# A Mamba block and a gated FFN on one core: the last batch's du*B of one group of four by GpSimd, the first batch's chain in halves, and a new order of all engines

## The chip, the cores and the metric

The kernel runs on one core of a Trainium2 chip, as one program of about 3400 instructions written by hand for each engine. The metric is the device time of one launch in microseconds (us): 197.79 us, the median of three runs (197.42 to 198.32). The engines are TensorE (PE, matrix products), VectorE (DVE), ScalarE (ACT), GpSimd (POOL) and SyncE (SP, which here issues all the DMAs).

## The reference

Four batches (BATCH = 4) of L = 256 tokens. The first layer is a Mamba block on a context of 128 features, with 256 inner channels, 16 states per channel and a convolution of 4 taps. Cut to what matters:

```python
x = einsum('bld,ed->bel', hidden_states, in_proj_w)
x = silu(causal_conv(x, conv_w) + conv_b)                 # u, 256 channels
dt_low, Bm, Cm = split(einsum('bdl,ed->bel', x, x_proj_w), [8, 24])
dt = softplus(einsum('brl,dr->bdl', dt_low, dt_proj_w) + dt_proj_b)
def step(state, inp):                                     # scan over the 256 tokens
    d, b, c, u = inp
    state = state * exp(d[..., None] * A) + (d * u)[..., None] * b[:, None, :]
    return state, einsum('bdn,bn->bd', state, c)
y = (scan(step) + D * x) * silu(z)                        # z = layernorm(x_in)
x_in = x_in + tanh(g_xattn) * swapaxes(y)
```

The second layer, on the sum, quantizes its layer norm per token to 8 bits, multiplies with `w13` (1408 x 256), forms `relu(x1)**2 * x3`, takes an RMS norm with weight, quantizes again, multiplies with `w2` (256 x 704), scales by tanh(g_ffn) and adds to the sum.

## The kernel before

The 256 inner channels are two halves (h = 0, 1) of 128 partitions; tokens lie along the free axis. The 16 states of a batch are worked in four groups, `k = 4 b + i` over the whole run. In batches 0 to 2 a group is 4 states on all 256 tokens. In batch 3 a group is 8 states on 128 tokens: groups 0 and 1 are tokens 0 to 127, groups 2 and 3 tokens 128 to 255, and the state at the cut is carried over (`edge`, `carry`).

Each group passes four engines, once for each half h, and these names stand for that everywhere below:

- `mixH` (PE, L959): du*B for all states of the group, written to PSUM (`m_ps`, two banks for each half and no second buffer), as a matmul of the transposed du with `bd`, diagonal blocks that hold B. In batches 1 to 3 `bd` is made by DMA: `bput` writes B's rows on the diagonal of a DRAM tensor, `bget` reads a group of it back (512 KB).
- `decayH` (ACT, L585): exp(dt*A) into `dA` (SBUF, two buffers).
- `scanH` (DVE, L783): the recurrence, from `dA` (SBUF) and `m_ps` (PSUM) into `hb` (SBUF, three buffers).
- `outH` (POOL, L356): hb times C, in place. C comes as `cs`, spread over all partitions by DMA (`cput` to DRAM, `cget` back, 512 KB a group).
- `sumH` (PE, L983): adds the states up in `y_ps` and transposes to tokens.

Ahead of a batch's groups runs the chain `ctxT`, `inproj` (PE), `tap` (ACT), `conv` (DVE), `sigm0` (ACT), `clamp` (DVE), `sigm1` (ACT), `u`, `xdbl` (PE), `lowc` (DVE), `dtproj` (PE), `absx`, `ln1q` (ACT), `series` (DVE), `cubic`, `dt` (DVE), `dtadd`, `du`, `duT` (PE and ACT), each on both halves in one instruction or one pair. After its groups come `yz`, `x1` (DVE) and the FFN: `center`, `absx1`, `quant1`, `xqT`, `up` (PE, L1013, 4 a batch), `relu`, `gate`, `gated`, `square`, `absmax`, `scale2`, `quant2`, `iqT`, `down` (PE, L1030), `final` and `store`. In batch 3 this is done for each 128 tokens alone. `w` are transposes of the FFN weights, with `w_hi`, `w_mid`, `w_res`, `w_lo` splitting each into three bf16 parts, and `warm` are PE transposes whose result is not used (L879).

Nothing is scheduled by a program: `PLAN` is a table written out by hand with one list for each engine, `name/batch.index` for each step, and each engine works its list strictly in order, waiting on semaphores. A step late in one list holds up all that stand behind it there. PE's outputs other than `m_ps` and `y_ps` share three PSUM banks in rotation (`claim`, `emptied`): a step waits until the one three fills ahead has been read.

```python
dve.wait_ge(dA_ok, HALVES * k + h + 1)
dve.wait_ge(m_full, HALVES * k + h + 1)
if k >= 3:
    dve.wait_ge(red_ok, HALVES * (k - 3) + h + 1)
```

## Time and profile before

| | |
|---|---|
| median of three runs | 197.79 us |
| the profiled execution: its time, its span | 197.55 us, 195.8 us |
| mean granted TensorE clock | 0.991 |
| PE, DVE, ACT, POOL busy | 177.1, 166.9, 152.2, 119.7 us |
| first scan starts, last matmul ends | 32.15 us, 193.03 us |

The profiled time is 1.75 us more than the span, which runs from the first to the last instruction. Busy time counts an engine's instructions alone; what it spends waiting for a semaphore is idle, and the rows show in brackets how long it was and who ended it. Matmuls are pipelined, so that a busy PE is one that has work in it. Rows of the timeline are merged stretches of like instructions and overlap by some tenths; rows of the chain are cut so that they do not. A fp32 matmul stands as two in the trace (x4 in a row is two of the program).

### The profile page before, as it was taken

What the parts mean: (1) busy time and instruction counts of PE and PEld (TensorE: products, weight loads), DVE (VectorE), ACT (ScalarE), POOL (GpSimd) and SP (SyncE); (2) the same over time, 40 slices, a digit from 0 to 9 for tenths busy, and PEclk for the clock granted to TensorE, in tenths of its full rate; (3) what the DMA queues carried; (4) which work ended last, traced back from release to release, by engine and by line L of the source; (5) the groups of instructions that cost most, each with busy time, mean ns of one, the idle gap of its engine ahead of it and who ended that gap; (6) DMA issues with size and microseconds to landing.
All of it is one profiled execution on the core that took longest, in us unless ns stands there. A gap on an engine that the chain in (4) does not pass through costs nothing.

```text
span 195.8 us, 3397 instructions
## 1 busy us (share of the span) xinstructions
PE 177.1 (90%) x1114; PEld 140.3 (72%) x1114; DVE 166.9 (85%) x260; ACT 152.2 (78%) x380; POOL 119.7 (61%) x83
## 2 busy tenths in 40 slices
...
GB/s 63 171 383 301 379 125 2 5 108 257 371 235 107 107 3 5 13 194 227 110 100 225 7 102 260 177 0 229 124 0 30 0 0 0 30 0 2 55 30 54
DMA packets 26498, 22.47 MB, mean 115 GB/s; under 512 B 15112, under 2 KB 19952, under 8 KB 26480
## 3 DMA queue, kind: packets, MB, share of 16 engines
...
## 4 chain that ended last, share of the span: by engine, by line
PE 52%; DVE 20%; issue 9%; POOL 9%; ACT 4%; SPq 2%; DMA 2%; DVEq 0%; POOLq 0%
PE m_ps L959 17%; PE w_ps L1013 12%; PE y_ps L983 10%; DVE hb L783 5%; POOL hb L356 5%; PE w_ps L1030 4%; DMA ctx_in<-in_ctx 2%; POOL dt L364 2%; PE w_ps L1021 2%; DVE gt L839 1%; POOL du L367 1%; PE w_ps L926 1%; PE w_ps L940 1%; POOL w13T L480 1%; PE y_ps L971 1%
## 5 line engine op out<-in xcount | busy, mean ns | idle before, releaser
L356 POOL TENSOR_TENSOR hb<-hb,cs 128x1024 f32<-128x1024 f32 x31 | 74.2, 2403 | 15.9 <-DVE hb L783 10.2
L783 DVE TENSOR_TENSOR_SCAN hb<-dA,m_ps 128x1024 f32<-128x1024 f32 x32 | 72.6, 2275 | 2.7 <-PE m_ps L959 2.0
L959 PE MATMUL m_ps<-bd,duT 128*128 128x256 f32 (+1 forms) x224 | 60.2, 413 | 2.3 <-issue 1.3
L585 ACT ACTIVATE dA<-dt,nega 128x255 f32<-128x255 f32 (+1 forms) x160 | 59.4, 452 | 0.0
L959 PEld LDWEIGHTS m_ps<-bd,duT 128*128 128x128 f32 x224 | 40.7, 190 | 14.1 <-issue 7.8
L983 PE MATMUL y_ps<-identf,hb 128*128 128x128 f32 x256 | 31.9, 273 | 2.4 <-POOL hb L356 2.4
L983 PEld LDWEIGHTS y_ps<-identf,hb 128*128 128x128 f32 x256 | 29.0, 141 | 5.1 <-POOL hb L356 2.8
L1013 PE MATMUL w_ps<-w13T,xqT 128*128 128x352 bf16 x192 | 30.4, 313 | 0.0
L1013 PEld LDWEIGHTS w_ps<-w13T,xqT 128*128 128x128 bf16 x192 | 18.6, 98 | 10.0 <-issue 0.9
L360 POOL TENSOR_TENSOR rr<-rr,q 128x512 f32<-128x512 f32 x2 | 2.9, 1470 | 24.1 <-DVE rr L739 24.1
L1030 PE MATMUL w_ps<-w2T,iqT 128*128 128x256 bf16 x144 | 16.7, 273 | 0.5 <-DVE ctx_in L856 0.5
L371 POOL TENSOR_TENSOR gw<-gg,normw 128x704 f32<-128x704 f32 x7 | 12.5, 1788 | 7.6 <-DVE gg L825 7.6
L705 DVE SCALAR_TENSOR_TENSOR xc<-w_ps,convw,xc 128x255 f32<-128x255 f32 (+2 forms) x24 | 9.6, 468 | 8.0 <-ACT xc L522 8.0
L1030 PEld LDWEIGHTS w_ps<-w2T,iqT 128*128 128x128 bf16 x144 | 13.8, 98 | 2.7 <-DVE ctx_in L856 0.8
L825 DVE SCALAR_TENSOR_TENSOR gg<-w_ps,finv,ru 128x352 f32<-128x352 f32 x16 | 9.0, 574 | 6.5 <-ACT ru L630 6.5
L627 ACT ACTIVATE ru<-w_ps,finv 128x352 f32<-128x352 f32 x16 | 8.7, 547 | 5.2 <-PE w_ps L1013 5.1
L646 ACT ACTIVATE iqT<-w_ps 128x384 bf16<-128x384 f32 x16 | 6.9, 481 | 4.1 <-PE w_ps L1021 4.1
L879 PE MATMUL y_ps<-identf 128*128 128x128 f32 x66 | 10.1, 314 | 0.0
L364 POOL TENSOR_TENSOR dt<-xs,lw 128x512 f32<-128x512 f32 x4 | 5.1, 1273 | 7.9 <-DVE lw L747 7.9
L879 PEld LDWEIGHTS y_ps<-identf 128*128 128x128 f32 x66 | 9.1, 165 | 0.7 <-issue 0.6
L620 ACT ACTIVATE xqT<-w_ps 128x512 bf16<-128x512 f32 (+1 forms) x5 | 2.5, 506 | 7.7 <-PE w_ps L1001 7.7
L630 ACT ACTIVATE ru<-ru 128x352 f32<-128x352 f32 x16 | 8.0, 497 | 0.5
...
## 6 DMA issues: line engine op xcount, KB each, us to landing
...
```

The source lines that it names most:

```text
L356: E.tensor_tensor(h_g, h_g, cs[:, s0:s0 + sn, l0:l0 + ln], ALU.mult).then_inc(hc_end if (b, i, h) == OUT_END else hc_ok[h], 1)
L364: E.tensor_tensor(dt[:, p], xs[:, :], lw[:, :], ALU.add).then_inc(dt_ok, 1)
L371: E.tensor_tensor(gw[:, p, i], gg[:, p, i], normw[:, :], ALU.mult).then_inc(gw_ok[i], 1)
L585: last = act_fn(dA_g[:, s, 1:ln], dt[:, p, h, l0 + 1:l0 + ln], ACT.Exp, scale=nega[:, h, s0 + s:s0 + s + 1])
L705: last = V.scalar_tensor_tensor(out=xc[:, h, s:L], in0=h_ps[:, h, 0:L - s], scalar=convw[:, h, TAPS - 1 - s:TAPS - s], in1=xc[:, h, s:L], ...
L783: V.tensor_tensor_scan(hb[:, k % 3, h], dA[:, k % 2, h].rearrange("p n l -> p (n l)"), m_ps[:, h], 0.0, ALU.mult, ALU.add).then_inc(scan_o ...
L825: V.scalar_tensor_tensor(out=gg[:, p, h, c * UC:(c + 1) * UC], in0=bank("up", b, i, 1)[:, 0:UC], scalar=finv[:, b, h:h + 1], in1=ru[:, p, ...
L879: T.transpose(y_ps[:, 0, 0:P], identf[:, :], identf[:, :])
L959: last = T.matmul(m_q[:, :, c * P - l0:(c + 1) * P - l0], duT[:, p, c, h * P:(h + 1) * P], bd[:, (s0 + sn // 2 * q) // GN, c, n0:n0 + sn / ...
L983: last = T.matmul(y_ps[:, t, h * P:(h + 1) * P], hb[:, k % 3, h, at:at + P], identf[:, :], start=False, stop=(s0 + s == NS - 1), is_transp ...
L1013: last = T.matmul(ps[:, 0:UC], xqT[:, kh, h, :], w13T[:, s, kh, c0:c0 + UC], start=(kh == 0 and s == 0), stop=(kh == 1 and s == 2))
L1030: last = T.matmul(ps[:, 0:DI], iqT[:, p, i, f, :], w2T[:, s, f * DI:(f + 1) * DI], start=(f == 0 and s == 0), stop=(f == FB - 1 and s == 2))
```

## The change

Three things change, and with the third nearly every line of the table.

1. Group 1 of batch 3 (8 states, tokens 0 to 127) loses its two mixes. SP writes 8 rows of B to DRAM (`mput`) and reads them back spread over all partitions (`mget`, two DMAs) into the part of `bd` that this group's diagonal blocks would have taken; the two `bget` of that part load half as much. POOL multiplies them with du into `hb` (`pm0`, `pm1`, 128x1024 each). ACT writes this group's decays into `m_ps` in place of `dA`, once the scan before has left it, and DVE scans from `m_ps` and `hb`, in place.
2. In batch 0 the chain from `inproj` to `duT` is cut into its two channel halves: `inproj/0.0`, `inproj/0.1` and so on for conv, clamp, u, dtproj, absx, ln1q, series, cubic, dt, dtadd, du, duT. Semaphores count with `tick`.
3. All five lists of `PLAN` stand in a new order.

The diff, cut to its core:

```diff
+PM = (None, None, None, 1)
...
+def by_pool(b, i):
+    return PM[b] == i
...
+def mixes(b, i, h):
+    return HALVES * sum((a, g) <= (b, i) and not by_pool(a, g) for a in range(BATCH) for g in range(NG)) + h - 1
...
+def halves(b, i):
+    return range(i, i + 1) if b == 0 else range(HALVES)
+def tick(b, i=HALVES - 1):
+    return i + 1 if b == 0 else HALVES + b
...
-        mix1/2.3 up/1.1 duT/3.0 up/1.2 down/0.0 mix0/3.0 mix1/3.0 up/1.3 szT/3.0 sum0/2.2 mix0/3.1 sum1/2.2 sum0/2.3
+        sum0/2.1 iqT/0.0 up/1.1 mix1/2.3 sum1/2.1 up/1.2 duT/3.0 sum0/2.2 mix0/3.0 up/1.3 mix1/3.0 sum1/2.2 sum0/2.3
...
+    b_dram = nc.dram_tensor("b_rows", (BATCH, NS, L), fp32, kind="Internal").ap()
...
+        def rows_of(b, i):
+            if b == BATCH - 1:
+                return bd[:, slots(b, i)[0]:slots(b, i)[-1] + 1, i // 2]
...
             elif name == "cubic":
-                eng.wait_ge(rr_ok, b + 1)
-                E.tensor_tensor(rr[:, :], rr[:, :], q[:, :], ALU.mult).then_inc(cubic_ok, 1)
+                eng.wait_ge(rr_ok, tick(b, i))
+                E.tensor_tensor(rr[:, hs], rr[:, hs], q[:, hs], ALU.mult).then_inc(cubic_ok, 1)
...
                 elif name == "bget":
                     sp.wait_ge(b_put, 16 * HALVES * b)
-                    sp.wait_ge(m_full, HALVES * (NG * (b - 1) + i + 1))
-                    sp.dma_start(bd[:, i], d_rows[:, :, GN * i:GN * (i + 1), :]).then_inc(b_got[i], 16)
+                    taken(b, i)
+                    cs_ = slice(0, HALVES)
+                    if b == BATCH - 1 and PM[b] is not None and i in slots(b, PM[b]):
+                        cs_ = slice(1 - PM[b] // 2, 2 - PM[b] // 2)
+                    sp.dma_start(bd[:, i, cs_], d_rows[:, cs_, GN * i:GN * (i + 1), :]).then_inc(b_got[i], 16)
+                elif name == "mput":
+                    s0, sn = group(b, PM[b])[2:]
+                    sp.wait_ge(free["dve"], emptied("xdbl", b, 0))
+                    sp.dma_start(b_dram[b, s0:s0 + sn], low[BROW + s0:BROW + s0 + sn, p, :]).then_inc(b_row[b], 16)
+                elif name == "mget":
+                    l0, ln, s0, sn = group(b, i)
+                    sp.wait_ge(b_row[b], 16)
+                    if b:
+                        for g in slots(b, i):
+                            taken(b, g)
+                    for g in range(sn // GN):
+                        sp.dma_start(rows_of(b, i)[:, g], b_dram[b, s0 + GN * g:s0 + GN * (g + 1), l0:l0 + ln]
+                                     .unsqueeze(0).broadcast_to([P, GN, ln])).then_inc(m_got, 16)
...
+                elif name in ("pm0", "pm1"):
+                    h = int(name[-1])
+                    l0, ln, s0, sn = group(b, i)
+                    pool.wait_ge(m_got, 16 * (before(b) + sn // GN))
+                    pool.wait_ge(du_ok, tick(b, h))
+                    if k >= 3:
+                        pool.wait_ge(red_ok, HALVES * (k - 3) + h + 1)
+                    nc.gpsimd.tensor_tensor(states(hb[:, k % 3, h], b, i).rearrange("p (g n) l -> p g n l", n=GN),
+                                            rows_of(b, i), du[:, p, h, l0:l0 + ln].unsqueeze(1).unsqueeze(1)
+                                            .broadcast_to([P, sn // GN, GN, ln]),
+                                            ALU.mult).then_inc(pm_ok, 1)
...
                 elif name in ("decay0", "decay1"):
...
-                    if k >= 2:
+                    if k and by_pool(b, i):
+                        act.wait_ge(scan_ok, HALVES * (k - 1) + h + 1)
+                    elif k >= 2:
                         act.wait_ge(scan_ok, HALVES * (k - 2) + h + 1)
...
+                    if by_pool(b, i):
+                        dA_g = states(m_ps[:, h], b, i)
...
                 elif name in ("scan0", "scan1"):
...
+                    if by_pool(b, i):
+                        dve.wait_ge(pm_ok, HALVES * before(b) + h + 1)
+                        V.tensor_tensor_scan(hb[:, k % 3, h], m_ps[:, h], hb[:, k % 3, h], 0.0, ALU.mult,
+                                             ALU.add).then_inc(scan_ok, 1)
+                        continue
-                    dve.wait_ge(m_full, HALVES * k + h + 1)
+                    dve.wait_ge(m_full, mixes(b, i, h))
...
                 elif name in ("mix0", "mix1"):
...
-                    pe.wait_ge(free["act"], emptied("duT", b, 0))
+                    pe.wait_ge(free["act"], emptied("duT", b, h if b == 0 else 0))
```

Three places of the order. On SP, the DMAs from the first `cput` on, in batch 0 and at the start of batch 1 (`cs<-c_rows` is `cget`, `b_diag<-low` is `bput`, `bd<-b_diag` is `bget`). Before:

```order
L409 DMA c_rows<-low 16x256
L429 DMA cs<-c_rows 128x1024
L419 DMA b_diag<-low 16x128x1 x2
L409 DMA c_rows<-low 16x256
L429 DMA cs<-c_rows 128x1024
L423 DMA bd<-b_diag 128x2x512
L429 DMA cs<-c_rows 128x1024
```

The same place now:

```order
L465 DMA c_rows<-low 16x256
L502 DMA cs<-c_rows 128x1024 x2
L476 DMA b_diag<-low 16x128x1 x2
L483 DMA bd<-b_diag 128x2x512
L465 DMA c_rows<-low 16x256
L483 DMA bd<-b_diag 128x2x512
L502 DMA cs<-c_rows 128x1024 x2
```

The second `cget` of batch 0 has moved ahead of `bput/1.0` and `cput/1.0`; the third and fourth now stand behind two `bget`.

On DVE, among the scans of batch 0 (`hb<-dA,m_ps` is a scan, `xc<-` is conv, `low<-` is lowc, `gg<-` is w_res, `rr<-rr,q` is cubic, `q<-rr,q` and `lw<-` are dt, `du<-dt,u` is du). Before, from the fifth scan of the run on:

```order
L783 SCALAR_TENSOR_TENSOR hb<-dA,m_ps 128x1024
L360 TENSOR_TENSOR rr<-rr,q 128x512
L716 TENSOR_TENSOR gg<-w_ps,w13T 128x512
L783 SCALAR_TENSOR_TENSOR hb<-dA,m_ps 128x1024
L745 SCALAR_TENSOR_TENSOR q<-rr,q 128x512
L747 SCALAR_TENSOR_TENSOR lw<-lw,lnsmall,q 128x512
L716 TENSOR_TENSOR gg<-w_ps,w13T 128x384
L783 SCALAR_TENSOR_TENSOR hb<-dA,m_ps 128x1024
L716 TENSOR_TENSOR gg<-w_ps,w2T 128x512
L367 TENSOR_TENSOR du<-dt,u 128x512
```

Now, from the first scan on:

```order
L883 SCALAR_TENSOR_TENSOR hb<-dA,m_ps 128x1024
L797 SCALAR_TENSOR_TENSOR xc<-w_ps,convw,xc 128x255 x2
L797 SCALAR_TENSOR_TENSOR xc<-w_ps,convw,xc 128x254 x2
L797 SCALAR_TENSOR_TENSOR xc<-w_ps,convw,xc 128x253 x2
L818 COPY low<-w_ps 80x256
L883 SCALAR_TENSOR_TENSOR hb<-dA,m_ps 128x1024 x4
L808 TENSOR_TENSOR gg<-w_ps,w13T 128x512
L833 TENSOR_SCALAR q<-q 128x512
L834 TENSOR_SCALAR rr<-q 128x512
L408 TENSOR_TENSOR rr<-rr,q 128x512
L840 SCALAR_TENSOR_TENSOR q<-rr,q 128x512
L842 SCALAR_TENSOR_TENSOR lw<-lw,lnsmall,q 128x512
```

`conv/2.0`, which stood right ahead of the first scan of batch 1, now stands behind the first scan of all, and series, cubic and dt of batch 1 follow each other with no scan between them.

On POOL, from du of batch 3 on (`hb<-hb,cs` is an out, `gw<-` is gated). Before:

```order
L367 TENSOR_TENSOR du<-dt,u 128x512
L356 TENSOR_TENSOR hb<-hb,cs 128x1024 x2
L371 TENSOR_TENSOR gw<-gg,normw 128x704
L356 TENSOR_TENSOR hb<-hb,cs 128x1024 x2
L351 TENSOR_TENSOR carry<-hb,edge 128x8
L356 TENSOR_TENSOR hb<-hb,cs 128x1024
L371 TENSOR_TENSOR gw<-gg,normw 128x704
L351 TENSOR_TENSOR carry<-hb,edge 128x8
```

Now:

```order
L415 TENSOR_TENSOR du<-dt,u 128x512
L404 TENSOR_TENSOR hb<-hb,cs 128x1024 x2
L419 TENSOR_TENSOR gw<-gg,normw 128x704
L404 TENSOR_TENSOR hb<-hb,cs 128x1024
L548 TENSOR_TENSOR hb<-bd,du 128x1024 x2
L419 TENSOR_TENSOR gw<-gg,normw 128x704
L399 TENSOR_TENSOR carry<-hb,edge 128x8
L404 TENSOR_TENSOR hb<-hb,cs 128x1024
```

`out0/2.2` has moved ahead of du (so three outs of batch 2 are left behind it, not four), and the two new products and `gated/1.1` stand between the last out of batch 2 and the first of batch 3.

## Rows read from the trace of the kernel before

**Rows 1.** The page, part 1: busy time of each engine, share, instructions.
```profile
PE 177.1 (90%) x1114; PEld 140.3 (72%) x1114; DVE 166.9 (85%) x260; ACT 152.2 (78%) x380; POOL 119.7 (61%) x83
```

**Rows 2.** Busy time by stage: stretch, length, each engine's busy us, clock, DMA.
```profile
0.00:30.00 30.00, 21.88 (x121) 17.30 (x121) 19.47 (x53) 18.32 (x40) 7.11 (x20) 0.94 0.68 232
30.00:60.90 30.90, 26.78 (x157) 22.65 (x157) 28.80 (x20) 26.30 (x60) 25.34 (x15) 1.00 0.58 166
60.90:122.90 62.00, 59.71 (x364) 49.76 (x365) 60.85 (x83) 56.59 (x132) 49.21 (x28) 1.00 0.48 113
122.90:180.00 57.10, 56.94 (x383) 41.64 (x382) 50.73 (x91) 45.19 (x138) 38.02 (x22) 1.00 0.13 47
180.00:195.80 15.80, 11.75 (x94) 8.91 (x92) 7.08 (x18) 5.79 (x14) 0.00 (x0) 1.00 0.13 43
```

**Rows 3.** The chain that ended last: start, us, engine, tile, line.
```profile
126.36 1.79 PE w_ps L1013 x12
...
136.65 1.72 PE m_ps L959 x4
...
152.26 0.87 PE y_ps L983 x8
153.13 0.66 PE w_ps L1021 x6
...
166.36 1.97 PE w_ps L1030 x18
```

**Rows 4.** Timeline of POOL: an out of batch 0, then batch 3.
```profile
44.77 2.36 POOL L356 TENSOR_TENSOR hb<-hb,cs 128x1024 f32<-128x1024 f32 x1 [5.24 <-DMA cs<-c_rows]
...
124.37 1.27 POOL L367 TENSOR_TENSOR du<-dt,u 128x512 f32<-128x512 f32 x1
...
139.41 1.69 POOL L371 TENSOR_TENSOR gw<-gg,normw 128x704 f32<-128x704 f32 x1
...
146.54 2.36 POOL L356 TENSOR_TENSOR hb<-hb,cs 128x1024 f32<-128x1024 f32 x1
154.36 2.52 POOL L356 TENSOR_TENSOR hb<-hb,cs 128x1024 f32<-128x1024 f32 x1 [5.46 <-DVE hb L783]
```

**Rows 5.** Timeline of DVE: scan0/3.1 and scan1/3.1.
```profile
138.46 2.29 DVE L783 TENSOR_TENSOR_SCAN hb<-dA,m_ps 128x1024 f32<-128x1024 f32 x1 [0.23 <-issue]
...
143.49 2.26 DVE L783 TENSOR_TENSOR_SCAN hb<-dA,m_ps 128x1024 f32<-128x1024 f32 x1
```

**Rows 6.** Timeline of PE: the last xqT.
```profile
179.99 0.38 PE L1001 MATMUL w_ps<-identf,xn 128*128 128x128 f32 x2
```

**Rows 7.** Timeline of PE: warm transposes behind the first dtproj.
```profile
17.84 2.39 PE L879 MATMUL y_ps<-identf 128*128 128x128 f32 x10
```

**Rows 8.** Timeline of DVE, first batch: start, us, line, [idle before, releaser].
```profile
32.15 2.29 DVE L783 TENSOR_TENSOR_SCAN hb<-dA,m_ps 128x1024 f32<-128x1024 f32 x1 [1.16 <-PE m_ps L959]
...
34.74 4.58 DVE L783 TENSOR_TENSOR_SCAN hb<-dA,m_ps 128x1024 f32<-128x1024 f32 x2
...
45.95 1.73 DVE L360 TENSOR_TENSOR rr<-rr,q 128x512 f32<-128x512 f32 x1
...
51.37 2.73 DVE L747 SCALAR_TENSOR_TENSOR lw<-lw,lnsmall,q 128x512 f32<-128x512 f32 x1
...
57.27 1.93 DVE L367 TENSOR_TENSOR du<-dt,u 128x512 f32<-128x512 f32 x1
...
63.64 2.27 DVE L783 TENSOR_TENSOR_SCAN hb<-dA,m_ps 128x1024 f32<-128x1024 f32 x1
```

**Rows 9.** Timeline of DVE, the same three instructions elsewhere.
```profile
25.15 0.75 DVE L747 SCALAR_TENSOR_TENSOR lw<-lw,lnsmall,q 128x512 f32<-128x512 f32 x1
...
83.52 0.69 DVE L360 TENSOR_TENSOR rr<-rr,q 128x512 f32<-128x512 f32 x1
...
88.88 1.14 DVE L367 TENSOR_TENSOR du<-dt,u 128x512 f32<-128x512 f32 x1
```

**Rows 10.** Timeline of DVE: a product of two columns in batch 0's FFN.
```profile
107.43 2.39 DVE L839 SCALAR_TENSOR_TENSOR gt<-gam,gsd 128x2 f32<-128x2 f32 x1
```

More of the change, by code:

```diff
@@ L80 @@
+        relu/2.0 relu/2.1 decay0/3.3 decay1/3.3 iqT/1.1 rs1/3.0 relu/2.2 center/3.0 relu/2.3 xqT/3.0 square/2.0
+        square/2.1 rs2/2.0 relu/3.0 relu/3.1 square/3.0 rs2/3.0 center/3.1 iqT/2.0 rs1/3.1 iqT/2.1 xqT/3.1 iqT/3.0
+        relu/3.2 relu/3.3 square/3.1 rs2/3.1 iqT/3.1
     """,
     "dve": """
-        conv/0.0 clamp/0.0 dtwT/0.0 xstat/0.0 u/0.0 xstat/1.0 xstat/2.0 lowc/0.0 xstat/3.0 conv/1.0 gates/0.0
-        series/0.0 clamp/1.0 w_res/0.0 w_res/0.1 dt/0.0 w_res/0.2 bd/0.0 bd/0.1 scan0/0.0 lowc/1.0 scan1/0.0
@@ L94 @@
-        scale2/3.0 quant1/3.1 outscale/3.0 quant2/3.0 final/1.1 final/2.0 gate/3.2 gate/3.3 gated/3.1 absmax/3.1
-        final/2.1 scale2/3.1 quant2/3.1 outscale/3.1 final/3.0 final/3.1
+        conv/0.0 conv/0.1 clamp/0.0 clamp/0.1 dtwT/0.0 u/0.0 xstat/0.0 u/0.1 xstat/1.0 lowc/0.0 conv/1.0 xstat/2.0
+        xstat/3.0 w_res/0.0 gates/0.0 series/0.0 w_res/0.1 series/0.1 dt/0.0 clamp/1.0 w_res/0.2 bd/0.0 dt/0.1
+        w_res/0.3 bd/0.1 scan0/0.0 conv/2.0 lowc/1.0 scan1/0.0 scan0/0.1 scan1/0.1 scan0/0.2 w_res/0.4 series/1.0
```

235 lines of the change are left out of this document (130 added, 105 removed).

## The prediction, made before the changed kernel was run

> **What bounds the kernel now.** I read the busy shares first, then the stages, then the chain, and last the timelines of the engines where the chain changes hands. The shares [rows 1] name PE as the fullest engine (177.1 us of 195.8) with DVE ten us behind it, which decides nothing: a share is an average over stages. The stages [rows 2] do. Up to 30 us no engine is full; this is a chain of single steps that hands from engine to engine. From 30 to 60.9 us DVE is busy 28.80 of 30.90 us and PE only 26.78: DVE bounds. From 60.9 to 122.9 both are dense (60.85 and 59.71 of 62.00). From 122.9 to 180.0 PE is busy 56.94 of 57.10 us, with 0.16 us of gaps, while DVE has 6.4 us idle, ACT 11.9 and POOL 19.1: here the end is set by how much work PE has. Behind 180.0 stands a tail that the chain passes through on PE, DVE and ACT by turns; its order on PE is the same before and now, so I move it as one piece. The reader should see one thing above all: a microsecond taken from PE's list behind 122.9 is a microsecond of the end, a microsecond taken from DVE between 30 and 123 is worth up to one as well, and one taken from POOL or ACT is worth none by itself.
>
> **Removed: two mixes of batch 3.** The chain cuts a mix of batch 3 at 1.72 us (the row at 136.65; the second, at 141.64, reads the same) [rows 3]. Both lie in the stretch where PE has 0.16 us idle. 2 x 1.72 = 3.44 us come off the path, if nothing is late in their place.
>
> **Added on POOL: pm0, pm1.** No row has this product, but an out is the same form, two fp32 inputs from SBUF, 128x1024 out: 2.36 us [rows 4]. One input of pm is spread from du, so its bounds are 1.27 x 2 = 2.5 us (du's own product has half the elements and takes 1.27) and 2.36; I take 2.4, so 4.8 us for both. Who hides it? POOL has 5.46 us idle before the out at 154.36, because scans of later groups come late [rows 4]. Step by step from the end of du/3.0 (125.64): three outs of batch 2 at 2.36, gated/1.0 at 1.69 as its like at 139.41, pm0 and pm1 give 125.64 + 7.08 + 1.69 + 4.8 = 139.2 [rows 4]. Scan0/3.1 and scan1/3.1 ran at 138.5 and 143.5 [rows 5], and pm0 is ready at 136.8, so neither scan waits for a product at today's times. The outs of batch 3 then shift: out1/3.1 ended at 148.90 (the row at 146.54 plus 2.36) and now ends at 153.7. Its sum1/3.1 stood at 152.3 on PE [rows 3], 27.7 us of PE work ahead of the xqT at 179.99 [rows 6]. In the new list less lies between: itself and four more sums, one mix, four `up`, three `iqT`, three `down`, a skip and an xqT. With 0.87 a sum, 1.72 a mix, 1.79 an up, 0.66 an iqT and 1.97 a down [rows 3], five sums make 4.35, the mix 1.72, four ups 7.16, three iqT 1.98, three downs 5.91, skip and xqT 0.67: 21.8 us. So POOL allows that xqT at 153.7 + 21.8 = 175.5, which is 4.5 us earlier than 179.99. The new products are hidden up to a gain of 4.5 us, and beyond it only if du/3.0 also comes earlier.
>
> **Added on ACT and DVE.** The decays of the group are 16 instructions of the same size as before, with PSUM as output, and now wait for the scan just ahead and no longer for the one before that. Today scan0/3.0 has ended before decay0/3.1 begins, so the stricter wait ends in time. The scan swaps which input is in PSUM. I price both at 0; bounds are -0.5 and +2 us (16 instructions of some 0.3 us, off by up to 0.12 each), and ACT's 11.9 us idle in this stage cover the plus end. mput and mget add three issues to SP, about 1.5 us, whose queue idles here; two bget load half.
>
> **The first batch in halves.** This shortens the chain where one half can go on while the other is worked, but the steps share queues. Taking rows at half size I get inproj's first half out 1 us earlier, but the second sigm0 still stands behind ctxT/1.0, which waits for its DMA. By that walk u ends 0.4 us earlier, lowc about 1.2 us. Then dtproj/0.1 stands behind the ten warm transposes (2.39 us [rows 7]) and two weight transposes, so that the second half's dt is about 2.7 us later than today while the first is 1.5 to 2 us earlier. DVE must also build both bd blocks, 4.6 us, ahead of its first scan. The first scan comes out at 31.5, against 32.15 [rows 8]: 0.65 us, which I do not count as the steps of this walk are good to no better than that. More DVE instructions (clamp, u, series, dt each once more) cost some 1.2 us on DVE, of which I take half, 0.6, as on the path.
>
> **New order, first batch.** The second cget of batch 0 stands in SP's list behind bput and cput of batch 1, and POOL waited 5.24 us for it [rows 4]. It now stands right behind the first, so that wait goes. What is late next: POOL will get to dtadd/1.0 before DVE has made dt/1.0, and wait there instead. That is worth nothing in itself, but it changes DVE: its three products of batch 1 are stretched while POOL works, 1.73, 2.73 and 1.93 us [rows 8], against 0.69, 0.75 and 1.14 for the same instructions elsewhere [rows 9]. The excesses are 1.04, 1.98 and 0.79, together 3.81. With POOL waiting for exactly dt, the 1.98 should go; of the other two I count none. The bounds of the head as a whole are 3.81 + 0.65 = 4.5 us gained, and a slip of the second half (a rival, below). I take 1.98 - 0.6 = 1.4 us. It reaches the end because DVE then runs dense to 122.9 with only 1.15 us idle [rows 2], and conv/2.0 has merely moved from ahead of scan0/1.0 to behind scan0/0.0, which is the same work.
>
> The Trainium skill ("SBUF — State Buffer", "Who interferes with whom") gives a rule for those stretched rows: GpSimd and a DVE instruction with two SBUF inputs share a pair of ports under an exclusive lock, and the loser waits for the whole instruction of the other. The trace agrees: the 2.73 us is 0.75 plus most of one out, and a product of two columns took 2.39 us [rows 10]. The rule also speaks against the change, since pm0 and pm1 are 4.8 us more of such locks; that is a rival with its own price below.
>
> **Sum.** 197.55 (the profiled execution, span 195.8) - 3.44 - 1.40 = 192.7. That execution lies 0.24 us under the median 197.79, so I forecast 193.0 us for the median, a span of about 191.0. The 4.84 us gained exceed POOL's 4.5 by 0.3, which asks du/3.0 to be 0.3 us earlier; with the 1.4 from the head it is.
>
> **Rivals.**
> 1. The gain is larger. All three stretched rows shrink and the first scan comes at 31.5: -3.44 - 4.5 gives 189.6 on this execution, 189.8 on the median. For it: POOL's idle moves to just this place. Against it: every engine is over 79% busy from 60.9 to 122.9, so little of a head's gain can pass unhurt.
> 2. The removed PE time comes back as waits. One more wait on POOL of the kind of the 5.24 us, say for cget/2.3, which now stands behind bput and bget of batch 3, puts out1/3.1 at 153.7 + 4 and the xqT at 179.5. Time 197.55 - 0.5 = 197.1, or 197.3 on the median: no change. For it: the strict lists, and a margin that is small by my count. Against it: in that stage POOL has 19.1 us idle, and its order was long enough ahead of PE before.
> 3. Slower. The second half of batch 0 comes so late that DVE stands in front of scan1/0.0. The new list puts conv/2.0 and lowc/1.0 ahead of scan1/0.0, on the far side of dtproj/0.1, absx/0.1, cubic/0.1, dtadd/0.1, du/0.1 and duT/0.1, each behind foreign steps in a queue (w_lo, u, sz on POOL; zsig on ACT). My walk has scan1/0.0 at 36.5, against 34.7 today [rows 8], with conv/2.0 already done. If three of these queues cost 2.4 us more each, DVE idles 7.2 us, of which the 1.4 and nothing else is returned: 197.55 - 3.44 - 1.4 + 7.2 = 199.9, or 200.1 on the median. It turns the sign by 0.5% once the slip exceeds 4.84 + 1.0 = 5.8 us. For it: DVE is 93% busy there, so that it cannot make it up. Against it: my walk leaves ACT and POOL some slack at each step.
> 4. The products lock out DVE. Each pm can hold one short DVE product for up to 2.39 us [rows 10], and quant1, scale2 and outscale of batches 1 and 2 stand right there. Two such blocks cost 4.8 us on DVE, which has 6.4 idle in the stage; half of that reaches PE through xqT/2.0 or the scans: 193.0 + 2.4 = 195.4.
> That the change doesn't do what it says can be excluded for the mixes: they are gone from PE's list.
>
> **How the numbers follow.** The forecast, with its own range of 191.0 to 195.0, gets 0.50; rival 1 0.10, rival 2 0.18, rival 3 0.13, rival 4 0.09. Below 190.2 lies half of rival 1, above 198.0 rival 3: 190.2 to 198.0 leaves out 0.18 and takes in the -0.5 and +2 of ACT and the head's bounds but for the slip. Within 0.5% of 197.79 (196.8 to 198.8, about what a measurement can tell from no change) lies most of rival 2, 0.14; above it 0.13; faster is the rest, 0.73.
>
> **What would show it.** PE busy near 173.6 us, with no m_ps matmul between scan0/3.0 and scan1/3.1. POOL without the wait for cs in batch 0 and with one for dt/1.0; DVE's L842 there at 0.75 and not 2.7. The first scan of batch 1 at 61 to 62.5, not 63.6. pm0 and pm1 at 2.4 us each, done before DVE asks. PE idle under 0.5 us in the 50 us ahead of the last xqT. I am wrong if PE has gaps in batch 3 ended by an out or a scan, if DVE idles in front of scan1/0.0, or if the first scan of batch 1 starts no earlier than 63.6.

## The result, and the profile after

The changed kernel takes 192.6 us (median of 4, 191.98 to 193.07) against 198.06 us for the kernel before on the same chip (4 runs, 197.42 to 199.7): a ratio of 0.971 (0.9642 to 0.9778). Forecast were 193.0 us, range 190.2 to 198.0. Run again on another chip it gave 0.9694 (0.963 to 0.9758). The profiled execution took 192.29 us with a span of 190.5, so 1.79 lie outside the span, as before (1.75). A profile shows one execution: those of runs 1, 6, 7, 8, 9 and 11 below are longer than is usual for their kernels, and in that of run 5 (209.5 us) the granted clock is at 8 tenths from the fifth slice on, so that from these only single waits, durations and the length of one stage are used, and whole times of any run only as ratios of usual executions.

The page, part 1, of the changed kernel, which answers to [rows 1]:

```profile
PE 176.2 (92%) x1106; PEld 140.8 (74%) x1106; DVE 164.3 (86%) x266; ACT 153.9 (81%) x389; POOL 122.5 (64%) x88
```

PE has eight matmuls fewer, 3.44 us on the chain, but is only 0.9 us less busy. Most of the difference is the clock: run 10 below has the same list on PE and the clock at full throughout, and there PE is busy 173.3 us. The granted clock in 40 slices of 4.76 us each (page, part 2):

```profile
PEclk9999699979999999999999999999999999999999
```

The fifth and the ninth slice are low. Before, one slice (14.7 to 19.6 us) stood at 7; here two do not stand at 9: 19.1 to 23.8, in the warm transposes, and 38.1 to 42.9, among the first mixes. The stages, in the columns of [rows 2], cut at 30 us, the first mix of batch 1, duT/3.0 and the last xqT:

```profile
0.00:30.00 30.00, 23.35 (x119) 18.38 (x119) 20.95 (x59) 21.65 (x51) 7.76 (x22) 0.94 0.74 247
30.00:57.89 27.89, 26.59 (x153) 22.66 (x152) 26.12 (x26) 24.67 (x57) 21.78 (x16) 0.94 0.46 135
57.89:123.72 65.83, 64.25 (x400) 53.60 (x399) 62.30 (x80) 60.53 (x144) 56.37 (x32) 1.00 0.39 109
123.72:175.38 51.66, 50.28 (x349) 37.26 (x346) 48.52 (x88) 41.28 (x127) 36.57 (x21) 1.00 0.21 70
175.38:190.50 15.12, 11.68 (x93) 8.94 (x92) 6.37 (x17) 5.74 (x14) 0.00 (x0) 1.00 0.11 36
```

I read the gain from three clock times. PE reaches the du transposes of batch 3 at 123.72, before at 125.70; these are the rows of its timeline, of after and then of before:

```profile
121.93 1.95 PE L1115 MATMUL w_ps<-w13T,xqT 128*128 128x352 bf16 x12
123.72 0.60 PE L1041 MATMUL w_ps<-identf,du 128*128 128x128 f32 x4
124.16 1.04 PE L1085 MATMUL y_ps<-identf,hb 128*128 128x128 f32 x8
```

```profile
125.70 0.66 PE L940 MATMUL w_ps<-identf,du 128*128 128x128 f32 x4 [0.16 <-POOL du L367]
...
127.98 2.13 PE L1030 MATMUL w_ps<-w2T,iqT 128*128 128x256 bf16 x18
```

It reaches the last xqT at 175.38 (the same row with xn, x2), before at 179.99 [rows 6]. By these marks 1.98 us come ahead of duT/3.0, 2.63 from the stage between the two (54.29 to 51.66 us) and 0.7 from the tail (15.8 to 15.1): 5.3 us of span. But duT/3.0 does not stand behind the same work in both lists. The new one has `up/1.2` right ahead of it (the row at 121.93), the old one right behind it (the 1.79 us at 126.36 in [rows 3]). Behind both steps PE stands at 124.16 now and at 127.98 before. Like for like the head therefore gives 3.82 us, the last stage only 0.79 (52.01 to 51.22 us) and the tail 0.69. From here on "stage 3" is this stretch from duT/3.0 to the last xqT.

The first batch on DVE, which answers to [rows 8] (start, us, line, [idle before, releaser]):

```profile
32.08 2.28 DVE L883 TENSOR_TENSOR_SCAN hb<-dA,m_ps 128x1024 f32<-128x1024 f32 x1
36.92 4.45 DVE L883 TENSOR_TENSOR_SCAN hb<-dA,m_ps 128x1024 f32<-128x1024 f32 x2
...
50.45 0.75 DVE L842 SCALAR_TENSOR_TENSOR lw<-lw,lnsmall,q 128x512 f32<-128x512 f32 x1
51.11 2.28 DVE L883 TENSOR_TENSOR_SCAN hb<-dA,m_ps 128x1024 f32<-128x1024 f32 x1
53.31 0.90 DVE L415 TENSOR_TENSOR du<-dt,u 128x512 f32<-128x512 f32 x1
...
59.88 4.46 DVE L883 TENSOR_TENSOR_SCAN hb<-dA,m_ps 128x1024 f32<-128x1024 f32 x2 [0.23 <-issue]
```

The first scan starts 0.07 us earlier, scan1/0.0 without idle time at 36.92, and the first scan of batch 1 at 59.88 in place of 63.64. The last two of the three stretched products are back at 0.75 and 0.90 us. POOL, in the places of [rows 4]:

```profile
51.28 1.26 POOL L412 TENSOR_TENSOR dt<-xs,lw 128x512 f32<-128x512 f32 x1 [4.19 <-DVE lw L842]
...
54.18 7.01 POOL L404 TENSOR_TENSOR hb<-hb,cs 128x1024 f32<-128x1024 f32 x3 [0.52 <-DMA cs<-c_rows]
...
121.57 1.44 POOL L415 TENSOR_TENSOR du<-dt,u 128x512 f32<-128x512 f32 x1
...
131.81 4.69 POOL L548 TENSOR_TENSOR hb<-bd,du 128x1024 f32<-128x1024 f32 x2 [0.20 <-DMA bd<-b_rows]
...
146.42 0.20 POOL L399 TENSOR_TENSOR carry<-hb,edge 128x8 f32<-128x8 f32 x1 [3.08 <-DMA cs<-c_rows]
```

The wait of 5.24 us for rows of C has become one of 4.19 us for DVE's L842, which POOL spends without holding anything. The two new products take 4.69 us and end at 136.50. The scans that read them, now with their decays in PSUM, follow at once:

```profile
136.63 4.46 DVE L872 TENSOR_TENSOR_SCAN hb<-m_ps,hb 128x1024 f32<-128x1024 f32 x2
```

At 2.23 us each they cost what a scan cost before [rows 5]. The first starts 0.13 us behind the end of the products' row, but it does not wait for it. It needs only `pm0`, done at about 134.16 (half of the row), and what stands right ahead of it on DVE is `final/0.0`, which starts at 136.26 and takes 0.45 us. The second starts at 138.86, 2.36 us behind `pm1`. So each product is done some 2.4 us before its scan. The gaps of PE in stage 3 are short ones:

```profile
126.49 1.12 PE L1061 MATMUL m_ps<-bd,duT 128*128 128x512 f32 x2 [0.36 <-DMA bd<-b_diag]
...
136.85 0.63 PE L1094 MATMUL w_ps<-identf,ze 128*128 128x128 f32 x4 [0.49 <-DVE ctx_in L956]
```

### The profile page after: what moved, and what is told of

Same layout as the page of the kernel before. It is cut to its first block, busy times and chain, and to the rows that moved or that the text cites. A ratio compares the mean times of both kernels' runs of the same rounds, so it can differ in the third digit from the quotient of the medians.

```text
span 190.5 us, 3413 instructions
## 1 busy us (share of the span) xinstructions
PE 176.2 (92%) x1106; PEld 140.8 (74%) x1106; DVE 164.3 (86%) x266; ACT 153.9 (81%) x389; POOL 122.5 (64%) x88
## 4 chain that ended last, share of the span: by engine, by line
PE 52%; DVE 23%; DMA 11%; issue 8%; SPq 4%; ACT 1%; DVEq 0%
PE m_ps L1061 20%; PE y_ps L1085 9%; PE w_ps L1115 8%; DMA bd<-b_diag 4%; DMA b_diag<-low 4%; PE w_ps L1132 3%; DMA x<-in_x 3%; PE y_ps L979 3%; DVE gg L925 2%; DVE bd L823 2%; DVE gam L930 2%; PE w_ps L1123 2%; DVE hb L883 2%; DVE xstat L848 1%; DVE x L893 1%
## 5 line engine op out<-in xcount | busy, mean ns | idle before, releaser
L404 POOL TENSOR_TENSOR hb<-hb,cs 128x1024 f32<-128x1024 f32 x31 | 72.9, 2368 | 2.2 <-DVE hb L883 1.4
L883 DVE TENSOR_TENSOR_SCAN hb<-dA,m_ps 128x1024 f32<-128x1024 f32 x30 | 67.8, 2275 | 4.4 <-PE m_ps L1061 1.6
L1061 PE MATMUL m_ps<-bd,duT 128*128 128x256 f32 (+1 forms) x216 | 57.9, 413 | 1.5 <-issue 1.1
L674 ACT ACTIVATE dA<-dt,nega 128x255 f32<-128x255 f32 (+1 forms) x144 | 54.5, 460 | 0.0
L1061 PEld LDWEIGHTS m_ps<-bd,duT 128*128 128x128 f32 x216 | 40.1, 194 | 10.7 <-issue 4.1
L408 POOL TENSOR_TENSOR rr<-rr,q 128x256 f32<-128x256 f32 (+1 forms) x3 | 3.0, 1001 | 20.3 <-DVE rr L834 20.3
L412 POOL TENSOR_TENSOR dt<-xs,lw 128x512 f32<-128x512 f32 (+1 forms) x5 | 5.4, 1076 | 11.3 <-DVE lw L842 11.3
L979 PEld LDWEIGHTS y_ps<-identf 128*128 128x128 f32 x66 | 9.6, 170 | 0.6 <-issue 0.5
L725 ACT ACTIVATE ru<-gg 128x704 f32<-128x704 f32 x8 | 6.2, 782 | 2.0 <-DVE gg L925 2.0
```

The lines of the kernel that those rows point to most:

```text
L404: E.tensor_tensor(h_g, h_g, cs[:, s0:s0 + sn, l0:l0 + ln], ALU.mult).then_inc(hc_end if (b, i, h) == OUT_END else hc_ok[h], 1)
L674: last = act_fn(dA_g[:, s, 1:ln], dt[:, p, h, l0 + 1:l0 + ln], ACT.Exp, scale=nega[:, h, s0 + s:s0 + s + 1])
L883: V.tensor_tensor_scan(hb[:, k % 3, h], dA[:, k % 2, h].rearrange("p n l -> p (n l)"), m_ps[:, h], 0.0, ALU.mult, ALU.add).then_inc(scan_o ...
L979: T.transpose(y_ps[:, 0, 0:P], identf[:, :], identf[:, :])
L1061: last = T.matmul(m_q[:, :, c * P - l0:(c + 1) * P - l0], duT[:, p, c, h * P:(h + 1) * P], bd[:, (s0 + sn // 2 * q) // GN, c, n0:n0 + sn / ...
```

## The experiments

The runs went to three chips, each with the kernel before beside it (medians 196.35, 196.57 and 196.70 us), so I compare ratios. Runs 9 to 12 were on the same chip.

### 1 and 2: the products alone, the order alone

Run 1 is the kernel before, in its order and with its whole chain, plus the products:

```
 pe:   sum0/2.2 [mix0/3.1] ... iqT/0.1 [mix1/3.1]      both mixes out
 pool: out0/2.3 out1/2.3 +pm0/3.1 +pm1/3.1 out0/3.0    (gated/1.0 stays ahead of out0/2.3)
 sp:   bget/3.2 cget/3.1 +mput/3.0 +mget/3.1 store/0.0
```

> Part one alone: the order of before and the whole (unhalved) chain, but group 1 of batch 3 made by GpSimd, its two mixes gone. Theory A, that the product needs the new order: the two products push out1/3.1 from 148.9 to 153.7 us, while the old order keeps 27.7 us of PE work behind sum1/3.1, so the last xqT can come no earlier than 181.4 against 180.0 of before. Expected 198 to 199.5 us, POOL without its 5.5 us wait, PE waiting 4 to 5 us for outs in batch 3. Rival B, that two mixes less on a dense PE are 3.4 us less whatever the order: 194.4 us.

Run 2 is the changed kernel without the products:

```
-PM = (None, None, None, 1)
+PM = (None, None, None, None)
 pe:   sum1/2.2 +mix0/3.1 sum0/2.3 ... down/0.0 +mix1/3.1 iqT/0.1
 pool: -pm0/3.1 -pm1/3.1      sp: -mput/3.0 -mget/3.1
```

> Parts two and three alone: the new order and the halved chain, with the two mixes back on PE (mix0/3.1 behind sum1/2.2, mix1/3.1 behind down/0.0) and no product on GpSimd. Theory A, PE dense in batch 3: 3.4 us more than the changed kernel, 196.0 us. Rival B, that the stage from duT/3.0 on now has idle time on PE (1.4 us in gaps and slow starts of 1.4 us more) which the mixes fill: 1.5 to 2.5 us more, 194 to 195 us. Rival C, that the product bought nothing: 192.6 us.

Run 1 gave 1.0212 (1.019 to 1.0235), slower than before and by more than its first theory had (2.1% are 4.2 us, expected were up to 1.7); run 2 gave 0.9864 (0.9822 to 0.9905). So the order with its halves is worth 1.4%, and the products are worth something only on top of it. In run 1 the timeline of DVE, then that of PE, shows why:

```profile
141.12 2.29 DVE L871 TENSOR_TENSOR_SCAN hb<-m_ps,hb 128x1024 f32<-128x1024 f32 x1 [1.06 <-POOL hb L547]
...
151.02 1.77 DVE L914 SCALAR_TENSOR_TENSOR fam<-fam,fsd 128x2 f32<-128x2 f32 x1
...
153.03 2.75 DVE L918 TENSOR_SCALAR xn<-xn,fs 128x256 f32<-128x256 f32 x2
```

```profile
144.85 0.76 PE L1072 MATMUL y_ps<-diag,u 128*128 128x128 f32 x4 [3.09 <-DVE x L892]
```

The product comes 1.06 us too late for its scan, what stands behind the scan on DVE comes late too, and PE, which has lost mix1/3.1 from exactly this place, waits 3.09 us for it, for DVE and not for an out as that theory had it. The 18 matmuls of the next `down` then take 3.79 us and not 2.13. Then two short instructions of DVE take 1.77 and 2.75 us beside POOL's outs, against 0.16 and 0.62 elsewhere. From duT/3.0 to the last xqT run 1 takes 57.71 us (127.53 to 185.24) where before took 54.29 with two mixes more. In run 2 stage 3 takes this long (columns of [rows 2]):

```profile
123.00:177.99 54.99, 53.92 (x356) 38.64 (x353) 49.72 (x88) 40.88 (x125) 31.98 (x19) 1.00 0.17 63
```

54.99 us with the mixes and 51.66 without them, at the same clock and in the same order: the products bring 3.33 us in this stage, and the forecast's term was 3.44. PE is 3.64 us less busy and has 0.3 more idle. The new order itself costs time here: behind duT/3.0 and up/1.2, run 2 takes 54.55 us to the last xqT (123.44 to 177.99) and the kernel before 52.01, for the same steps.

### 3: batch 0's chain whole

The changed kernel with halves(), tick() and all steps x/0.1 of the chain taken out; the whole steps stand where the first halves stood.

```
-    return range(i, i + 1) if b == 0 else range(HALVES)
+    return range(HALVES)
```

> The changed kernel with the first batch's chain whole again, each pair of half steps made one step at the place of the first half. Theory A, the halves bring little: the first scan started at 32.08 against 32.15 of before, so the time is 192.2 to 193.5 us. Rival B, that the halves are what brings the first scan of batch 1 forward (59.9 against 63.6): 195 to 196.5 us.

It gave 0.9977 (0.995 to 1.0004): 2.9% more than the changed kernel's 0.9694, nearly all of the gain, and more than either theory allowed. The first scan comes at 37.43 us and not at 32.08; stage 3 is no longer than elsewhere, 50.89 us. DVE's timeline:

```profile
34.98 2.35 DVE L823 TENSOR_TENSOR bd<-identf,w_ps 128x1024 f32<-128x1024 f32 x2 [2.09 <-PE w_ps L1032]
37.43 2.29 DVE L883 TENSOR_TENSOR_SCAN hb<-dA,m_ps 128x1024 f32<-128x1024 f32 x1
```

DVE stands 2.09 us for PE, which had itself stood 2.50 us for DVE's weight residues. This list is written for halves: whole steps in the places of first halves block both queues. It doesn't show that halves beat whole steps in an order of their own, since before the whole chain had its first scan at 32.15 [rows 8]. It shows that the halves and the order can't be priced apart.

### 4 and 5: the head of the kernel before, mended by hand

Run 5 moves one transfer in the kernel before; run 4 does this too and puts DVE's series, cubic and dt of batch 1 together, with du/1.0 earlier and POOL waiting for dt, as in the changed kernel.

```
 run 5, sp:   cget/0.0 +cget/0.1 bput/1.0 cput/1.0 -cget/0.1
 run 4, also: dve  scan1/0.1 scan0/0.2 w_res/0.4 series/1.0 cubic/1.0 dt/1.0 scan1/0.2 du/1.0 w_res/0.5 ...
              pool out1/0.1 w_lo/0.3 dtadd/1.0 out0/0.2 out1/0.2
```

> The kernel before with two pieces of the new order only: the second cget of batch 0 right behind the first, and on DVE series, cubic and dt of batch 1 in a row while GpSimd waits for dt (dtadd/1.0 moved ahead of out0/0.2). Theory A: DVE's three products of batch 1 fall from 1.73, 2.73 and 1.93 us to 0.7, 0.75 and about 1, the first scan of batch 1 starts 2.5 to 3.8 us earlier, and the time is 194.5 to 196 us. Rival B, that the rest of the old order gives the gain back before the end: the scan starts earlier, the time stays at 197.3 to 198.

> The kernel before with one DMA issue moved: the second cget of batch 0 right behind the first. Theory A: GpSimd's 5.24 us wait for cs goes, but GpSimd does not bound there, so the time changes by less than 0.5%: 197 to 198.5 us. Rival B, that this wait was on the way to the end: 194 to 196 us.

Run 5 gave 0.9925 (0.9899 to 0.9952), run 4 0.9965 (0.9953 to 0.9977). The first of batch 1's scans comes at 61.27 us in run 4, 2.4 earlier than before; two of the products are mended (0.69 and 0.75) but du takes 2.10. By the ratio little reaches the end: 0.35% are 0.7 us. The two traces say otherwise: in that of run 4 duT/3.0 comes at 123.62 and the last xqT at 177.92, 2.08 and 2.07 us earlier than before, by the same list on PE. But the trace of before is of an execution of 197.55 us, and beside run 4 that kernel's median is 196.35. So the ratio counts, and how much of the 2.1 us is the edit's stays open.

The transfer moved alone, the smaller edit, gains at least as much; the two intervals just miss each other, and the runs were on two chips. Run 5's profile shows that POOL's wait of 5.24 us is gone by this move alone, and that the three products then take 0.66, 0.75 and 1.06 us, while another short one (L739) takes 2.46 for its 0.43. What the other edit gives back, and where, these runs don't tell.

### 6 and 7: the wait of 3.08 us taken away

POOL's 3.08 us for the last rows of C come from SP's list, where cget/3.3 stands behind two stores. Run 6 moves it ahead of them; run 7 moves lowc/3.0 ahead of outscale/0.0 on DVE too.

```
 run 6, sp:  cget/3.2 +cget/3.3 store/0.0 store/0.1 -cget/3.3
 run 7, also dve: quant1/1.0 +lowc/3.0 outscale/0.0 -lowc/3.0
```

> The changed kernel with the last cget ahead of the two stores of batch 0. It goes after the 3.08 us that GpSimd waited for cs ahead of out0/3.1. Theory A: that wait is hidden (sum0/3.1 did not wait for it on PE), so the time stays within 0.3 us of the changed kernel, 192.3 to 192.9. Rival B: it was on the way, 190.5 to 191.5 us.

> As the kernel with the last cget moved, and lowc/3.0 ahead of outscale/0.0 on DVE, so that the rows of B of batch 3 leave about 0.9 us earlier. The chain lowc, cput, bput (6.9 us to landing), bget (8.1 us) ended in PE's wait before mix0/3.0. Theory A: the wait of 0.4 us there goes and the mixes start at full pace, 0.5 to 1 us less than the changed kernel: 191.6 to 192.1. Rival B: du and duT of batch 3 come last anyway, no change: 192.6.

Both were slower, which none of their theories had: 1.0051 (1.0024 to 1.0077) and 1.0187 (1.0128 to 1.0246), where the changed kernel has 0.9694. In run 6 the wait is gone, and this is what POOL, DVE and PE do at that place. POOL:

```profile
147.24 2.35 POOL L403 TENSOR_TENSOR hb<-hb,cs 128x1024 f32<-128x1024 f32 x1
...
149.82 2.34 POOL L403 TENSOR_TENSOR hb<-hb,cs 128x1024 f32<-128x1024 f32 x1
```

DVE:

```profile
147.24 2.35 DVE L914 SCALAR_TENSOR_TENSOR fam<-fam,fsd 128x2 f32<-128x2 f32 x1
...
149.83 2.74 DVE L918 TENSOR_SCALAR xn<-xn,fs 128x256 f32<-128x256 f32 x2
```

PE:

```profile
152.63 1.11 PE L1102 MATMUL w_ps<-identf,xn 128*128 128x128 f32 x4 [4.29 <-DVE xn L918]
...
154.82 5.35 PE L1114 MATMUL w_ps<-w13T,xqT 128*128 128x352 bf16 x24
```

Two short instructions of DVE begin in the very moment in which POOL begins a product, and the first ends with it: 2.35 us. The second row is two instructions, one of which sits out the product: 2.74 us. In the changed kernel POOL is standing for rows of C just then, and the same two take 0.16 and 0.62:

```profile
143.59 0.16 DVE L915 SCALAR_TENSOR_TENSOR fam<-fam,fsd 128x2 f32<-128x2 f32 x1
...
143.99 0.62 DVE L919 TENSOR_SCALAR xn<-xn,fs 128x256 f32<-128x256 f32 x2
```

The two locks cost 4.3 us on DVE, PE stands for 4.29, and then its granted clock is at 6 and 7 tenths for two slices, so that 24 matmuls take 5.35 us and not 3.74. Stage 3 takes 57.45 us (127.61 to 185.06) against 51.66. By the ratios the whole of run 6 is 3.7% over the changed kernel, 7 us, and that stage alone shows 5.8. A wait that looked like waste was the gap through which DVE's chain went. Scans are not held: they run beside POOL's products throughout at 2.3 us. The Trainium skill ("SBUF — State Buffer", "Who interferes with whom") has this as a lock on a shared pair of ports, for which the loser waits through the whole instruction of the other; the rows agree, down to the instruction's end.

### 8 and 10: the products twice, and not at all

Run 8 makes each product twice. Run 10 leaves the products out: a copy of 8 columns stands in their place, and that group's scans read whatever the buffer holds.

```
-    nc.gpsimd.tensor_tensor(states(hb...), rows_of(b, i), du[...]...broadcast_to(...), ALU.mult).then_inc(pm_ok, 1)
+    run 8:  the same twice, then_inc on the second
+    run 10: nc.gpsimd.tensor_copy(hb[:, k % 3, h, 0:8], rows_of(b, i)[:, 0, 0, 0:8]).then_inc(pm_ok, 1)
```

> The changed kernel with each of GpSimd's two products made twice, the same values: 4.7 us more on GpSimd ahead of out0/3.0. Theory A, that the products are hidden with little to spare (GpSimd waits 3.1 us for cs and DVE takes scan0/3.1 at 136.6, when the second product is made): 1.5 to 3 us more, 194.1 to 195.6, with PE waiting for scans or outs of batch 3. Rival B, that GpSimd has room for them: less than 0.5 us more.

> The changed kernel with its two products on GpSimd left out: a copy of 8 columns each stands in their place, so the scans of that group read what is in the buffer. This part of the computation is left out. Theory A (GpSimd's two products, 4.69 us together, cost the end little, as their DVE scans come only 5 us later): 0 to 0.8 us faster than the changed kernel on the same chip. Rival B (they hold up GpSimd's later products, and DVE's short operations beside them, so that their time is paid): 2.5 to 4.5 us faster. Rival C (without them GpSimd runs ahead and meets DVE's short chain of the third batch, as when its wait for the rows of C was taken away): 1 to 5 us slower.

Run 10 gave 0.9706 (0.9653 to 0.9759) beside the changed kernel's 0.9694 on the same chip: leaving 4.69 us of POOL out gains nothing that these intervals of 0.6% to each side could show. POOL's 4.4 us saved turn into waits (timeline of POOL, run 10):

```profile
134.87 0.20 POOL L399 TENSOR_TENSOR carry<-hb,edge 128x8 f32<-128x8 f32 x1 [2.31 <-ACT edge L677]
...
144.65 0.21 POOL L399 TENSOR_TENSOR carry<-hb,edge 128x8 f32<-128x8 f32 x1 [4.54 <-DMA cs<-c_rows]
```

Stage 3 takes 51.14 us there (122.49 to 173.63), as in run 9 with the products in. Run 8 gave 1.0151 (1.0112 to 1.0191), 4.7% over the changed kernel: 9 us for 4.7 us more on POOL, where its first theory had at most 3. Its DVE:

```profile
140.76 2.29 DVE L875 TENSOR_TENSOR_SCAN hb<-m_ps,hb 128x1024 f32<-128x1024 f32 x1 [0.96 <-POOL hb L549]
145.51 2.29 DVE L875 TENSOR_TENSOR_SCAN hb<-m_ps,hb 128x1024 f32<-128x1024 f32 x1 [2.46 <-POOL hb L549]
...
150.07 2.17 DVE L918 SCALAR_TENSOR_TENSOR fam<-fam,fsd 128x2 f32<-128x2 f32 x1
```

3.4 us of waits for the products, then three such locks (2.17, 2.21 and 2.37 us). In these two runs POOL's work costs nothing while it ends before the scan that reads it, and more than its own length beyond. The changed kernel has some 2.4 us to spare: run 8 puts 4.7 us ahead of the second scan, which waits 2.46.

### 9, 11 and 12: the changed kernel again, and two single moves in it

Run 9 is the changed kernel as it is. Run 11 moves lowc/3.0 on DVE ahead of outscale/0.0 (the second move of run 7 alone). Run 12 puts cget/0.1 back:

```
 run 12, sp: cget/0.0 -cget/0.1 bput/1.0 bget/1.0 cput/1.0 +cget/0.1 bget/1.1
```

> The changed kernel itself, again, so that the kernels of this call have it on their own chip. Theory A (two causes: the new order with the halves gives about 1.4%, the products on GpSimd another 1.5%): the ratio to the kernel before is again about 0.971, 0.965 to 0.978. Rival B (the kernel with the new order and the mixes on TensorE, measured at 0.986 on another chip, was as fast as the changed kernel, and the difference lay in the chips): 0.980 to 0.988.

> The changed kernel with one move on DVE: the copy of the rows of B and C of the last batch (lowc/3.0) goes ahead of outscale/0.0. Theory A (the first wait of TensorE in the last stage is that for the diagonals, which start from this copy): about 0.4 us faster than the changed kernel, as TensorE waits 0.36 us for them. Rival B (the rows of C come earlier too, GpSimd loses its wait of 3.08 us for them and locks DVE's short operations out, as in the run with cget/3.3 ahead of the stores): 2 to 5 us slower. Rival C: nothing to see, within 0.3%.

> The changed kernel with one move on SP: cget/0.1, the rows of C for the second group of the first batch, goes back behind bput/1.0, bget/1.0 and cput/1.0. Theory A (this wait was a part of what the first batch lost, and the one move in the kernel before gave 0.75%): GpSimd waits 3 to 4.5 us for these rows ahead of out0/0.1, and the kernel is 0.5 to 1.5% slower than the changed kernel on the same chip. Rival B (in the new order scan0/1.0 is set by DVE's own list and the wait is made up within the first batch): within 0.3%.

Run 9 gave 0.9694, on a second chip, so the difference to run 2 is hardly one of chips, though no chip had both: the intervals, 0.963 to 0.9758 and 0.9822 to 0.9905, lie apart. The products are worth 1.7% on the new order.

Its profile shows how little the changed kernel's list needs to lose time. From 28 to 64 us the rows of DVE and PE stand within 0.1 us of those in the first profile. Then DVE's clamp/2.0, first in the first profile, then in run 9:

```profile
64.26 0.42 DVE L390 TENSOR_SCALAR sg<-sg 128x512 f32<-128x512 f32 x1
```

```profile
64.34 2.64 DVE L390 TENSOR_SCALAR sg<-sg 128x512 f32<-128x512 f32 x1
```

It starts 0.08 us later, in the moment in which POOL begins an out, and takes 2.64 us; duT/3.0 then comes at 126.02, 2.30 us later than in the first profile. So where the head ends differs between two executions of the same kernel by more than the forecast's whole term for it. Whether such locks make the spread of the changed kernel's times isn't shown.

Run 11 gave 0.9955 (0.9915 to 0.9995), 2.7% over the changed kernel. That is 5.1 us, at the upper end of the second theory's range, but its mechanism is not what happened: POOL still waits 3.0 us for the rows of C. The time goes in batch 2, 20 us earlier. DVE's timeline in run 11:

```profile
108.04 0.42 DVE L817 COPY low<-w_ps 80x256 f32<-80x256 f32 x1 [0.62 <-PE w_ps L1017]
108.38 1.14 DVE L774 TENSOR_SCALAR gv<-ssq 128x2 f32<-128x2 f32 x1
109.56 2.27 DVE L775 TENSOR_TENSOR gos<-grs 128x2 f32<-128x2 f32 x1
...
112.51 4.47 DVE L882 TENSOR_TENSOR_SCAN hb<-dA,m_ps 128x1024 f32<-128x1024 f32 x2
```

and in the changed kernel:

```profile
108.10 0.22 DVE L947 SCALAR_TENSOR_TENSOR gos<-gt,gates,grs 128x2 f32<-128x2 f32 x1
108.36 0.42 DVE L818 COPY low<-w_ps 80x256 f32<-80x256 f32 x1
108.70 4.45 DVE L883 TENSOR_TENSOR_SCAN hb<-dA,m_ps 128x1024 f32<-128x1024 f32 x2
```

The copy waits 0.62 us for PE. The four small steps of outscale/0.0 thereby come 1.1 us later, into POOL's products that start at 108.23 and 109.46; two of them, on two columns, take 1.14 and 2.27 us, and the scans start 3.81 us later. PE then runs out of work and comes back at the lower clock (PE, run 11):

```profile
114.90 6.62 PE L1060 MATMUL m_ps<-bd,duT 128*128 128x256 f32 x16 [3.36 <-issue]
```

The same 16 matmuls start at 111.69 and take 3.62 us in the changed kernel: 3.21 us later and 3.00 longer, and duT/3.0 is 6.22 us later (129.94). Stage 3 behind it is untouched, 51.01 us. So a 0.62 us wait became 3.8 us by the lock and 6.2 by the clock. Run 7, which has this move too, shows the same rows (0.62 of wait, then 1.13 and 2.27).

Run 12 gave 1.0081 (1.0042 to 1.0121), 4.0% over the changed kernel, beyond both theories' sizes. The wait on POOL was to be 3 to 4.5 us:

```profile
50.72 4.65 POOL L404 TENSOR_TENSOR hb<-hb,cs 128x1024 f32<-128x1024 f32 x2 [8.81 <-DMA cs<-c_rows]
55.33 1.26 POOL L412 TENSOR_TENSOR dt<-xs,lw 128x512 f32<-128x512 f32 x1
```

It is 8.81 us, as a bget of 512 KB now goes ahead of the cget too, and dtadd/1.0 stands behind the outs that it holds. DVE:

```profile
56.63 1.63 DVE L415 TENSOR_TENSOR du<-dt,u 128x512 f32<-128x512 f32 x1 [4.70 <-POOL dt L412]
```

In the order before, du/1.0 stood behind a scan of the last group; now it stands ahead of both, so DVE stands 4.70 us for it, the granted clock is at 8 and 7 tenths from 49.7 to 59.6 us, and the du transposes of batch 3 come at 129.99, 6.3 us late.

## Why the prediction was right, step by step, and where by luck

- **Two mixes off the path, -3.44.** Right. At equal order stage 3 shrinks from 54.99 to 51.66 us, by 3.33; in runs 9 and 10 it takes 51.14. Nothing late took the place of the mixes. But the forecast gave the term to the products alone, and run 1 shows that in the old order they lose 2%.
- **The new order of the last stage, 0 in the sum.** This is what the forecast had wrong. For the same steps but the two mixes, the kernel before takes 52.01 us to the last xqT and the changed one 51.22. With 3.44 for the mixes, 2.65 us are lost there, about half as idle time of PE (1.38) and half as more busy time for the same matmuls, at a granted clock of 1.00. Run 2 has the mixes and loses 2.54 in the same place, so the order does it and not the mixes' absence.
- **The products, 2.4 us each, hidden.** 2.35 us each. Done at 136.50 for a forecast of 139.2, as du/3.0 came 2.8 us earlier. Run 10: their cost is nil. The forecast's limit, that POOL allows the last xqT no earlier than 175.5, fits 175.38 by luck, for the outs ended 1.8 us ahead of its count (151.9 for 153.7). The forecast had both products ready ahead of their scans, by 1.7 and 4.3 us; measured were 2.5 and 2.4.
- **Decays into PSUM, 0.** Right: 2.23 us a scan.
- **The halves, first scan at 31.5, +0.6 on DVE.** The scan came at 32.08. That I didn't count these 0.65 us was right, but that the halves cost as much as they bring was a walk through a mixed list, and run 3 shows such a walk prices nothing: this order needs them.
- **The order of the first batch, -1.98.** The mechanism was as forecast: POOL waits 4.19 us for exactly dt, L842 is at 0.75 us. The size was too low, as the other two products are short as well (0.69 and 0.90): 3.76 us at scan0/1.0, near the upper bound of 4.5. Like for like all of it is left in batch 3 (3.82 behind duT/3.0 and up/1.2), which bears out that a dense DVE passes a gain of the head on; the term of the sum, -1.4, was 2.4 short. The clock cost a part even so: the mixes at 39.30 and 42.83 took 2.88 and 2.28 us, and in run 10, where the clock stayed up, 1.97 and 1.91, together 1.28 less, and there duT/3.0 comes at 122.49, 1.23 earlier. In run 9 a lock of 2.2 us takes more than half of the head's gain away again.
- **The whole.** Forecast 4.84 us less, measured 5.26 on the profiled executions (197.55 to 192.29), with the tail's 0.7, most of it the end of a wait of iqT/3.0 (0.58), uncounted. That the total fits so well is in part luck: the head gave 2.4 us more than its term and the last stage 2.65 less, and the two errors cancel. Two of the forecast's own signs tell of this. Under 0.5 us idle was forecast in stage 3 and 1.38 came, so the reading of a dense PE list was too clean. PE busy 173.6 was forecast and 176.2 came; here the clock did most, as run 10 has 173.3.
- **The rivals.** Rival 1 (189.8) failed, though its premise nearly held: three shortened products and 3.82 of its 4.5 us in the head, with the first scan at 32.08 and not 31.5. What it lacked was the last stage's loss. Rival 2 (a wait on POOL of the kind of 5.24 us) came true as a wait, 3.08 us for cget/3.3 and not for cget/2.3, but cost nothing, since it freed DVE. Rival 3 failed: no idle time ahead of scan1/0.0. Rival 4 as written failed: in the 4.69 us of the two products DVE has a scan, yz/2.0, x1/2.0 with its statistics and final/0.0, each as long as in run 10, where the products are out; quant1, scale2 and outscale come behind them. But its mechanism, with outs in place of the products, was the best of the rivals: that it doesn't happen hangs on that wait and on a hair's breadth in batch 2 (DVE's last small step starts at 108.10, POOL's product at 108.20), and in runs 6, 7 and 11 it eats most or all of the gain. I gave it 2.4 us on PE; in run 6 it costs stage 3 5.8 us and in run 11 duT/3.0 6.2, as PE's clock falls behind the gap.

**What stays open.** Whether run 4 really gains less than run 5, and why. Which steps of the new order cost the last stage its 2.65 us: the three longest gaps of PE (0.36, 0.49 and 0.28 us) are 1.1 of it. What the halves are worth by themselves. And whether POOL's last products could be put so that DVE gets its gap without a wait; neither of the two moves tried beat the changed kernel, and no version faster than it was found.
